# A transformer block with mixture of experts: the router reads rows before they are normalised, and the first expert's weights are split later

## The reference, cut to what matters

```python
x = x + tanh(g_xattn[0]) * xattn(layernorm(x), ctx)     # both factors rounded to fp8 by blocks, then einsum
x = x + tanh(g_ffn[0]) * moe(layernorm(x), Wg, w1, w2)
# moe: S = 2048 rows of d = 512, E = 8 experts of 2048 hidden columns, top 2, at most C = 640 rows each
probs = softmax(xr @ Wg);  gate_vals, expert_idx = top_k(probs, 2)
# rows take slots of their expert in order; a row past slot C is dropped
h = relu(einsum('ecd,edf->ecf', dispatched, w1));  expert_out = einsum('ecf,efd->ecd', h, w2)
out = sum over the two of gate * expert_out
```

## Time and profile before

| what | value |
|---|---|
| median of 3 runs | 901.55 us (901.01 to 903.36) |
| the profiled execution | 899.0 us, its span 897.2 us |
| TensorE busy | 822.8 us, 92% of the span |
| VectorE, ScalarE, GpSimd busy | 643.1, 365.4, 196.5 us |
| mean granted TensorE clock | 0.975 |

### The profile page before, as it was taken

The page is one execution under the profiler, slowest core; times in us unless marked ns, Lnnn a source line. Parts: engine busy times, 40 slices in busy tenths (PEclk is TensorE's granted clock), DMA queues, the critical chain, the costliest instruction groups (busy, mean ns, idle before and its releaser), DMA issues.

```text
span 897.2 us, 13430 instructions
## 1 busy us (share of the span) xinstructions
PE 822.8 (92%) x4809; PEld 400.3 (45%) x4810; DVE 643.1 (72%) x1119; ACT 365.4 (41%) x587; POOL 196.5 (22%) x165
## 2 busy tenths in 40 slices
PE   0287989499999999999999999999999999999996
PEld 0134558344444444444444444444444444444443
DVE  5999868768596877788688578857885878585530
ACT  3798996334133441444043414331432144224410
POOL 2132331500232023203220232023202320232001
PEclk9999996599999999999999999999999999999999
DMA  8600734382456266328542763265328532702000
GB/s 302 260 0 1 259 116 171 93 290 95 125 163 211 101 145 234 123 94 175 219 147 98 129 223 123 105 145 211 120 97 169 206 123 94 175 24 70 1 26 22
DMA packets 77753, 123.05 MB, mean 137 GB/s; under 512 B 41870, under 2 KB 41886, under 8 KB 73632
## 3 DMA queue, kind: packets, MB, share of 16 engines
q1 hardware_dynamic: 68032, 93.33, 32.4%
q0 software_dynamic: 9696, 29.39, 11.4%
HBM read 96.49 MB, written 18.87 MB: 129 GB/s over the span
## 4 chain that ended last, share of the span: by engine, by line
PE 80%; DVE 10%; ACT 4%; DMA 2%; issue 2%; POOL 1%; SPq 0%; DVEq 0%; POOLq 0%; ACTq 0%
PE mm L750 37%; PE mm L817 36%; PE mm L790 2%; PE mm L729 2%; PE marks_ps L578 1%; ACT region L874 1%; DVE region L1183 1%; DVE region L1194 1%; DVE region L1225 1%; DVE region L1221 1%; DMA gains<-in_g_ffn 1%; POOL region L448 1%; DMA w_stage<-in_L_ffn_w 1%; PE mm L521 1%; PE mm L549 1%
## 5 line engine op out<-in xcount | busy, mean ns | idle before, releaser
L817 PE MATMUL mm<-region,w_split 128*128 128x512 f16 x1536 | 347.7, 380 | 1.7 <-ACT region L971 1.4
L750 PE MATMUL mm<-region 128*128 128x512 f16 x1536 | 335.8, 379 | 0.0
L750 PEld LDWEIGHTS mm<-region 128*128 128x128 f16 x1536 | 148.2, 98 | 179.7 <-issue 4.5
L817 PEld LDWEIGHTS mm<-region,w_split 128*128 128x128 f16 x1536 | 142.3, 98 | 159.8 <-issue 3.8
L1102 ACT ACTIVATE region<-mm 128x512 f16<-128x512 f32 x128 | 76.4, 597 | 323.3 <-PE mm L817 323.3
L1534 DVE SCALAR_TENSOR_TENSOR region<-mm,region 128x512 f16<-128x512 f32 x128 | 88.5, 691 | 88.1 <-ACT region L1102 88.1
L461 POOL DMA_INDIRECT out<-region,back_now x40 | 64.9, 1623 | 168.6 <-DVE region L1547 141.3
L1537 DVE SCALAR_TENSOR_TENSOR region<-w_stage,w_scale,region 128x512 f16<-128x512 f32 x128 | 96.5, 754 | 0.0
L1105 ACT ACTIVATE region<-w_stage,w_scale 128x512 f16<-128x512 f32 x128 | 91.2, 712 | 0.0
L438 POOL PARTITION_ALL_REDUCE peak_all<-peak x14 | 4.9, 349 | 352.9 <-DVE peak L1292 299.1
L1312 DVE TENSOR_REDUCE top<-w_stage 128x1 f32<-128x512 f32 x112 | 75.9, 678 | 2.9 <-DMA w_stage<-in_L_ffn_w 2.9
(11 more groups left out here) (188 smaller groups left out, 620.9 us busy)
## 6 DMA issues: line engine op xcount, KB each, us to landing
w_stage<-in_L_ffn_w SPq DMA_DIRECT2D x64, 1024.0 KB, 5.4
region<-in_x SPq DMA_DIRECT2D x4, 1024.0 KB, 13.4
x_split<-region SPq DMA_DIRECT2D x8, 512.0 KB, 3.8
out<-region SPq DMA_DIRECT2D x4, 1024.0 KB, 7.4
w_stage<-in_ctx SPq DMA_DIRECT2D x2, 1024.0 KB, 12.4
region<-in_ctx SPq DMA_DIRECT2D x2, 1024.0 KB, 15.5
region<-x_split,row_next POOLq DMA_INDIRECT x40, 4.5
region<-out,row_next POOLq DMA_INDIRECT x40, 3.8
```

What stands on the lines that cost most here:

```text
L750: mm = pe.matmul(mm2[s % 2][:, :], hidden[:, hh, f, s * P:(s + 1) * P], w2_split[:, wh, f, :], start=(f == 0 and hh + wh == 0), stop=(f == ...
L817: mm = pe.matmul(products(f), w1_split[:, wh, k, f * P:(f + 1) * P], xT[:, xh * KD + k, 0:WIDE], start=(k == 0 and wh + xh == 0), stop=(k ...
```

## The change

The router's matmuls read turned rows of `x_all` as `residual` leaves them, instead of normalised ones. The mean is taken off by the weights: `sum_router` on TensorE adds the router's weights over all 512 rows, `even_router` on VectorE subtracts the mean (`wg_even`), and `take_logits` on VectorE multiplies the logits of a group by `rstd_b` in place of ScalarE's copy. `turn_norm` waits for `prod_read` (the residual) and no longer for `xn_ready`. Four semaphores become one per context each. The handwritten orders of all four engines are new. All four `split_w1(0, ..)` stand behind `first_columns(3)`, the four `low_w1(0, ..)` behind `list_loads`, and TensorE waits for each high and low half inside f = 0. `keep_busy` issues 22 matmuls whose result nobody reads. New `copy_turned`, `copy_norm` and `halve` for VectorE are defined and not called.

```diff
-                    pe.wait_ge(q["xn_ready"], i + 1)
+                    pe.wait_ge(q["prod_read"], i + 1)
-                    need(pe, q["xnT_ready"], i - 1)
+                    bank_read(i, xnT_ready)
-                        mm = pe.transpose(turn_ns[m % 2][:, k, :], xn[:, m, k * P:(k + 1) * P], ident32[:, :])
+                        mm = pe.transpose(turn_ns[m % 2][:, k, :], x_all[:, i, k * P:(k + 1) * P], ident32[:, :])
...
+            def sum_router():
+                pe.wait_ge(q["const_base"], 1)
+                pe.wait_ge(q["consts_in"], 48)
+                for k in range(KD):
+                    mm = pe.matmul(wg_sums, ones32, wg_sb[:, k, :], start=(k == 0), stop=(k == KD - 1))
+                mm.then_inc(q["wg_summed"], 1)
...
+            def even_router():
+                dve.wait_ge(q["wg_summed"], 1)
+                V.scalar_tensor_tensor(wg_even[:, :, :], wg_sums.unsqueeze(1).broadcast_to([P, KD, E]), -1.0 / D,
+                                       wg_sb[:, :, :], ALU.mult, ALU.add).then_inc(q["wg_ready"], 1)
+            def take_logits(g):
+                tiles = slice(*GROUPS[g])
+                dve.wait_ge(q["logits_done"], GROUPS[g][1])
+                V.tensor_tensor(logits[:, tiles, :], logits_of(g)[:, tiles, :], over(rstd_b[:, tiles], E),
+                                ALU.mult).then_inc(q["logits_read"], 1)
...
             def expert(e, last):
-                pe.wait_ge(q["w1_lo"], e * KD + KD)
...
+                            if f == 0 and wh + xh == 0:
+                                pe.wait_ge(q["w1_hi"], e * KD + k + 1)
+                            if f == 0 and wh == 1:
+                                pe.wait_ge(q["w1_lo"], e * KD + k + 1)
```

More of the change, by code:

```diff
@@ L679, in _ @@
+            attend(2, [2])
+            attend(2, [3])
             router(2, [0])
+            turn_x(3, [0])
+            router(2, [1])
             turn_norm(2, [2])
             turn_norm(2, [3])
-            router(2, [1])
+            sums(1)
+            turn_x(3, [1])
+            attend(3, [0])
             router(2, [2])
+            turn_x(3, [2])
+            attend(3, [1])
+            turn_x(3, [3])
             router(2, [3])
+            attend(3, [2])
+            place(0)
+            attend(3, [3])
@@ L1009, in _ @@
             down(1, [2])
             down(1, [3])
-            copy_turned(1, [1])
+            row_mag(2, 0)
+            square(0, 3)
+            centre(3)
+            root(0)
+            copy_norm(0, [0])
+            row_mag(2, 1)
+            copy_turned(1, [2])
+            copy_turned(1, [3])
+            copy_norm(0, [1])
+            context_mag(2)
+            normalise(0, [0])
+            normalise(0, [1])
             down(2, [0])
             down(2, [1])
-            copy_turned(1, [2])
@@ L1029, in _ @@
-            halve(0, 0)
+            copy_norm(1, [0])
+            copy_norm(1, [1])
+            up(3, 0)
+            up(3, 1)
+            copy_turned(2, [0])
+            square(1, 0)
             row_mag(3, 0)
+            copy_turned(2, [1])
+            row_mag(3, 1)
+            root(1)
+            context_mag(3)
             copy_turned(2, [2])
-            root(1)
-            up(3, 1)
-            halve(0, 1)
-            copy_norm(0, [2])
-            row_mag(3, 1)
-            context_mag(3)
@@ L1038, in _ @@
-            copy_norm(0, [3])
-            down(3, [0])
+            copy_norm(1, [2])
             normalise(1, [0])
             normalise(1, [1])
+            normalise(1, [2])
+            normalise(1, [3])
+            copy_norm(1, [3])
+            copy_norm(2, [0])
+            down(3, [0])
             copy_turned(2, [3])
+            square(1, 1)
+            copy_norm(2, [1])
+            square(1, 2)
+            square(1, 3)
             down(3, [1])
-            copy_norm(1, [0])
-            normalise(1, [2])
@@ L1046, in _ @@
-            copy_norm(1, [1])
-            square(1, 0)
-            normalise(1, [3])
-            split_w1(0, 0)
-            square(1, 1)
-            copy_turned(3, [0])
-            square(1, 2)
-            copy_turned(3, [1])
             halve(1, 0)
             halve(1, 1)
+            copy_turned(3, [0])
             down(3, [2])
+            copy_norm(2, [2])
             down(3, [3])
-            square(1, 3)
-            copy_norm(1, [2])
+            root(2)
+            copy_norm(2, [3])
@@ L1485, in _ @@
             residual(2, [1])
+            first_scale(0)
+            round_rows(3, 1)
+            take_logits(0)
+            round_context(3)
             residual(2, [2])
-            round_context(3)
             residual(2, [3])
             norm_var(2)
-            round_rows(3, 1)
-            residual(3, [0])
             norm_scale(2)
@@ L1494, in _ @@
             first_scale(1)
+            choose(0)
+            residual(3, [0])
+            take_logits(1)
+            choose(1)
             residual(3, [1])
+            first_places(0)
             residual(3, [2])
```

290 lines of the change are left out of this document (143 added, 147 removed).

## The result

| | before | after |
|---|---|---|
| median of 5 runs | 901.42 us (900.21 to 903.36) | 907.45 us (906.74 to 908.53) |
| profiled execution | 899.0 us, span 897.2 | 907.3 us, span 905.5 |
| TensorE, VectorE, ScalarE, GpSimd busy | 822.8, 643.1, 365.4, 196.5 us | 830.6, 646.2, 365.1, 190.2 us |

What follows compares the result with a forecast made beforehand. No engine is full in the preparation, order binds; what counts is when the first expert gets into its stride. -3.8 (preparation) - 4.4 (gathers) + 9.25 (weights' halves) = +1.05 us, so 902.6 us; range 896.5 to 907.5.

Steps and rivals of the forecast that it cites:

- Rival B: TensorE's clock falls during the third and fourth contexts: two attends of 7.2 instead of 3.6 us, +4.8, 907.4 us; 22%.
- Rival C: Gathers issue as slowly without the low halves beside them, so nothing is gained there: +4.4, 907.0 us; 6%.
- Piece 2: From index list `row_next` to the last turned tile: gathers issue alone, 11.3 us instead of 15.7, gain 4.4 us.
- The rule that spoke against it: VectorE locks GpSimd out only in 2-port modes, impossible for two-tensor L1321; low halves would not slow gathers, gain 0.
- Piece 3: From T (end of `first_columns(3)`) to the fifth product's start: late weight halves, 23.2 against 13.95 us, loss 9.25 us.
- Piece 1: Preparation up to the index list `row_next` in its new order: list at 159.3 instead of 163.16, counted as -3.8 us.
- the second root's wait: In the preparation VectorE stands idle 2.8 us for ScalarE's `root(2)`, after 4.6 us for `root(1)`.
- Rival A: VectorE's waits for `root(1)` and `root(2)` are not there: list up to 5.3 us sooner, 897.3 us; 28%.
- D: Delayed halves cost less, f = 1 at full clock and its one-hot in time: 1.65 + 1.3 less, 899.6 us; 4%.
- `keep_busy` at 0: Its 22 matmuls stand in gaps where TensorE waits, so they cost 0.

Runs made afterwards that it cites:

- `changed_again`: The changed kernel unchanged, run again: 905.55 us, ratio 1.0047 to the kernel before.
- `low_rows_vector`: The changed kernel with `low_rows(2)` on VectorE as two halves instead of on GpSimd: 921.62 us, ratio 1.0133 to the kernel before.
- `changed_two_cures`: The changed kernel with `low_rows(2)` on VectorE, high halves ahead of `first_columns`, low halves behind GpSimd's fifth gather: 913.74 us, ratio 1.0058 to the kernel before.
- `before_again`: The kernel before, unchanged, run again for its trace: one run, 903.74 us.
- `no_filler`: The changed kernel without `keep_busy`'s 22 matmuls: 924.49 us, ratio 1.0172 to the kernel before.
- `router_alone`: The kernel before with only `sum_router`, `even_router`, `turn_norm` on `x_all` and `take_logits`, engine orders otherwise as before: 901.34 us, ratio 1.0008.

## Why the prediction was right and wrong

The range holds the result by 0.05 us, and that is luck. The forecast was 902.6, with 899.6 to 905 as its own range, and the time came out 4.85 us above. The upper edge of 907.5 stood there for rivals B and C. C's mechanism was not there, and B's figure of 907.4 needed two attends of 7.2 us, where one took 5.37.

- **Piece 2** (-4.4): right in mechanism and nearly in size, -5.0. The first issue alone took 1.19 us and not 0.95. The fourth gather landed 3.7 us after its issue, sooner than the 4.5 of the earlier trace rows. The rule that spoke against it was outweighed by the row, and the runs decide for the row: with the low halves beside it the first issue takes 2.67 us, without them 1.19, and the third takes 2.90 against 0.95. The section of the Trainium skill cited in the prediction (DMA: Bandwidth & Descriptors, SWDGE vs HWDGE vs iDMA) names a 2-port mode and does not say that nothing else locks GpSimd out. Another page of the Trainium skill (SBUF — State Buffer, SBUF: two separate sides) has the lock taken by a VectorE instruction with two SBUF inputs as well, against GpSimd work that reads SBUF. L1321 has two such inputs, and the stretched issues agree.
- **Piece 3** (+9.25): right, +9.8 in the profile and +8.9 in `changed_again`. The term that varied is f = 1 at the low clock, 4.4 predicted, 5.19 and 4.3 measured. What the prediction said of the loads holds: SP issues them at 181.95, T + 4.46, when the first low half has ended (T + 4.35 predicted). It did not see that in the kernel before they wait for SP's turn behind the fifth tile's transfer, long after `w1_lo`. That changed nothing after, but by it the mark of the kernel before varies by nearly 5 us.
- **Piece 1** (-3.8): wrong, +3.6. The step that failed is "From 125.6 VectorE has 33.6 us of work without another long wait." From the end of the second root's wait (128.44) to the list's end it took 38.35 us. Of the 4.7 us more, 3.3 are L1388 beside `low_rows(2)`, a term that the sum had at nothing. The other 1.4 are about what VectorE waited in short pieces: 0.8 us for TensorE (the slow attend above all) and 0.7 for ScalarE. The router's last products were done at 154.99, not 146.4, and VectorE, late itself, waited only 0.17 us for them. `low_rows_vector` takes the hold away and gets 1.4 to 2.2 us back, net of the 2.4 us of low rows that VectorE then does; `changed_two_cures` gets nothing back. The other 2.8 us of the miss lie ahead: 1.5 up to `norm_var(1)` (ScalarE's first instruction waited for the gains until 12.51 instead of 10.75, and the stretch shifts with it), and 1.4 from there to the end of the second wait. The first is not the change's doing as far as two runs can tell: in `before_again` that instruction waited until 12.00, and the list is at 164.46, 1.3 later than in the first profile. ScalarE's list up to `root(1)` adds up to 25.65 us, not 25.8, which changes nothing.
- **The price that was missed was to be seen before.** The trace of before has the hold, in small; here beside `context_down`, VectorE and GpSimd:

```profile
116.79 1.76 DVE L1255 TENSOR_SCALAR var_eps<-mv 128x4 f32<-128x4 f32 x1
```

```profile
114.91 3.61 POOL L396 TENSOR_TENSOR region<-region 128x2048 f32<-128x2048 f32 x1 [7.92 <-DVE region L1225]
```

Both end near 118.5; the same form of L1255 took 0.17 in the earlier trace rows. The Trainium skill (SBUF — State Buffer, SBUF: two separate sides) states this direction of the lock: of GpSimd's instruction and one of VectorE in a 2-port mode or with two SBUF inputs, whichever starts first keeps the shared ports for its whole instruction. The traces agree: L1175, with two inputs, takes 3.42 us instead of 0.16, and L1388, with one, 3.50 instead of 0.18 (the profile doesn't show its mode), each ending within 0.05 us of GpSimd's.
- **Rival A** (waits not there) fell twice: they were there, and without them a hold of 3.4 us appears. **Rival B** (the clock) came true in small and as a consequence, one attend of 5.37 us after a wait of 3.42. It cost the list at most the 0.67 us that VectorE waited for that attend. **Rival C** fell. **D** did not occur.
- `keep_busy` at 0 agrees with `no_filler`, indirectly; the router's new form at about 0 stands by `router_alone` (+0.6 us, its interval holds 1).

## What to carry to other kernels

Before moving short VectorE instructions, look for what GpSimd runs beside them: a wait in front of such an instruction can be cover for a hold of GpSimd's, and then costs little to keep and brings nothing to remove. Work that the matrix engine needs first, such as the first weights' halves, is worth its place in the preparation even if it slows a transfer: here 5 us gained on the gathers cost 9 to 10 on the first products. And follow a load to the queue that issues it: the semaphore it waits for may have been ready long before the queue's turn came.

## What the runs showed of the hardware

- Two short instructions of VectorE (L1388, `TENSOR_SCALAR` 128x32 with one input, and L1175, `TENSOR_TENSOR` 128x4 with two) take 0.16 to 0.2 us alone and 3.4 to 3.5 us when GpSimd's `TENSOR_TENSOR` of 4.07 us has started before them; they end with GpSimd's. Not every form is held. A reduce of one input (L1387, 0.42 us) and a reciprocal (L1174, 128x4, 0.18 us) beside the same GpSimd instruction were not, nor was a `TENSOR_SCALAR` on one number a partition in the kernel before (L1255, 128x1, 0.15 us at 139.51, beside GpSimd from 136.43 to 140.51). L1155 behind it, with two inputs, was: 0.40 us, up to GpSimd's end.
- Chips differ: before took 901.4 and 900.8 us in two measurements, 909.2 and 908.2 on two other chips, with some 8 us more from the fifth product on in the kernels traced there (712 to 713 against 704.3).
- On the second kind ScalarE stood idle for 10 to 18 us until 1.9 to 2.1 us after GpSimd's tenth gather issue, in all seven kernels with quick issues, and VectorE for 12 to 14 us in four of them, until within 1.1 us of that issue's end. What they wait for the profile doesn't name, and no run here tells. That it goes with the chip's kind rests on two chips against one or two, each used at one time only.
